# Attention probabilities of a fused two-layer block: turned by way of DRAM and 32x32 blocks instead of on TensorE

## The chip, the cores and the metric

One core of a Trainium2 chip. The metric is the device time of one execution in microseconds (us), as the median over runs. The engines are TensorE (PE in the profile, its weight loads PEld), VectorE (DVE), ScalarE (ACT), GpSimd (POOL) and SyncE (SP, which here only issues DMA).

## What is computed

Two layers over 1024 tokens (16 sequences of 64) of width 512, everything in fp32. Cut to what matters, the reference is:

```python
x = x + L0_xattn(layernorm(x), ctx, ctx)        # linear attention, 8-wide heads
x = x + L0_ffn(layernorm(x))                    # low-rank gated FFN
x = x + L1_xattn(layernorm(x), ctx)             # 16 heads of 96, 4 KV heads, 64 queries x 128 keys
x = x + L1_ffn(layernorm(x))                    # 16 experts, top 4, and a shared expert
# L1_xattn, per sequence b:
scores = einsum("bkgqd,bksd->bkgqs", q, k) / sqrt(96)
attn   = softmax(scores, axis=-1)
out    = einsum("bkgqs,bksd->bkgqd", attn, v)
return out_rows @ Wo.T
```

The change lies in L1_xattn, between the softmax and the product with the values.

## The kernel before, in words

All engines walk through one list of steps, `prog` (lines 296 to 420), and each emits its own part of each step, in the list's order. There is no scheduler at run time: what stands ahead of a wait on an engine delays what stands behind it.

The second attention is cut into 32 **units** n = 2b + hf: sequence b, half hf of the KV heads, that is 8 heads of 64 queries and 128 keys as four 128x128 tiles u. One turn of the loop at line 389, here called iteration n, puts these steps in this order:

```python
("s", n); ("gate_v", ..); ("kv", ..) for n < 7; ("sh_gu", ..) for n in 25, 29, 32
("pn", n); ("q", q + 1, r // 2) for even n < 24; way(n, 0)
("t", n - 1); way(n, 2); ("pv", n - 2); way(n, 1)
```

- `s` (n): TensorE multiplies queries and keys into PSUM bank 2 or 3 (L1451). VectorE takes the row maxima (L1114, L1116), ScalarE the exponentials with their row sums (L798, four instructions) into `prob`.
- `pn` (n): VectorE inverts the sums and multiplies (L907, L908).
- `t` (n - 1), one iteration later: TensorE turns the four 128x128 tiles of `prob` (L1458, through the helper line L1273) into a PSUM bank, and ScalarE copies the bank to `probT` (L803 to L806, helper line L700).
- `pv` (n - 2), two iterations after the scores: TensorE multiplies the values with `probT` (L1466, L1467) into bank 6. VectorE copies the product to `oT` with two copies of 96x192 (L1130) and three of 32x128 (L1132).
- `kv` (L1362 to L1371) projects keys and values in iterations 0 to 6. TensorE waits there until ScalarE has copied the previous projection (L1345; copies L758 to L765).
- `q` (L1433 to L1437) projects queries. ScalarE copies three heads (L789), VectorE the fourth (L1105).
- `way` (L370 to L384) spreads the output projection (`op0`, `opm`, `op1`, L1482), the third layer norm (`ln_stat`, `ln_z`; for five of eight token blocks VectorE turns 32x32 blocks, L1078, and ScalarE moves them, `ln_m`, 16 copies of 32x128 at L743), the router (`gate`, `gate_v`) and the placing of rows (`place`) over later iterations.
- `sh_gu` is the shared expert's first product. Its first one, in iteration 25, waits for the weights `wsh` (L1513).

SP's queue in this stage: it loads `wo` in two halves (L536, L538), then waits until all of Q is done (`s_q`, L539) and loads `wsh` (L540, 1.5 MB). It waits for the router's first result, and for all scores (L544), and loads the first two experts' weights (L546, helper line L443); then it waits for the placed rows and loads the first block of them (L455).

The second layer norm of the layer before is already turned by way of DRAM (`turn_rows`, L516 to L525): SP stores 128 rows (L519), waits for the store to land, and issues four loads of 64 KB that put each quarter of the columns onto its own 32 partitions (L524), and VectorE turns 32x32 blocks (L1083).

After the list, a loop over some 36 blocks of rows runs the experts.

Of the kernel before, what the change touches and what calls it, by code (L numbers as in the profile page):

```python
# [13 lines left out]
P = 128  # L14
# [24 lines left out]
def build(nc, x_d, ctx_d, ctxT_d, cst_d, u1_d, v1_d, u2_d, v2_d, b1_d, b2_d,  # L39
# [7 lines left out]

    id_d = nc.dram_tensor("slots", (P, 2 * P), F32, kind="Internal").ap()

    with ExitStack() as stack:  # L50
# [8 lines left out]
        cst = sb("cst", [P, 4 * P + 224])  # L59
# [9 lines left out]
        c0 = 4 * P  # L69
# [12 lines left out]
        prob = r1[:, 6144:7168].rearrange("p (n u s) -> p n u s", n=2, u=4)  # L82
# [87 lines left out]
        idrow = sb("idrow", [P, P, 2])  # L170
# [69 lines left out]
        s_pn = sem("probs_done")  # L240
        s_o = sem("pv_done")
# [187 lines left out]
        TRN = order(("a_t", "ln_t", "t", "gate", "front", "place", "count"))  # L429
# [44 lines left out]
        def _(sp):  # L474
# [22 lines left out]
            sp.dma_start(cst[:, 2 * P:], cst_d[:, 2 * P:]).then_inc(s_tables, 16)  # L497
# [39 lines left out]
            sp.wait_ge(s_pr, len(KVN))  # L537
            load_wo(1)  # L538
            sp.wait_ge(s_q, 4 * G)  # L539
            sp.dma_start(wsh, ws_d).then_inc(s_ws, 16)  # L540
# [29 lines left out]
        def _(pool):  # L570
# [27 lines left out]
            for step in prog:  # L598
                if step[0] == "a_stat":
                    root(step[1])  # L600
                elif step == ("f_in", 0):
                    pool.wait_ge(s_tables, 16)
                    pool.tensor_copy(counters[:, :], cst[:, 2 * P:4 * P]).then_inc(s_cb, 1)
                elif step[0] == "x1":
                    j = step[1]
                    pool.wait_ge(s_ac, j + 1)
                    pool.tensor_tensor(xr[:, j, :], xr[:, j, :], sout, ALU.add).then_inc(s_x1, 1)
                elif step[0] == "ln_stat":
                    root(J * step[1] + step[2])
                    if step[1] == 3 and step[2] >= J - 2:  # L610
                        place_ids(step[2] - 2)
                elif step[0] == "ln_z" and step[1] == 1:
                    j = step[2]
                    if j == 0:
                        pool.wait_ge(s_ffw, 6 * 16)
                    pool.wait_ge(s_z, LNN[step] + 1)
                    pool.tensor_tensor(xr[:, j, :], xr[:, j, :], b2, ALU.add).then_inc(s_xb, 1)
                elif step[0] == "place":
                    j = step[1]
                    pool.wait_ge(s_sl, j + 1)  # L620
                    if j == 0:
                        pool.wait_ge(s_idz, 16)
                        pool.wait_ge(s_fill, 5 * 16)
                    pool.wait_ge(s_z, LNN[("ln_z", 3, j)] + 1)
                    for k in range(TOPK):
                        if j:
                            pool.wait_ge(s_zs[k], 16 * j)
# [59 lines left out]
        def _(act):  # L687
# [15 lines left out]
            for step in prog:  # L703
# [88 lines left out]
                elif kind == "s":  # L792
                    n = step[1]
                    act.wait_ge(s_snm, n + 1)
                    if n >= 2:
                        act.wait_ge(s_tr, TRN[("t", n - 2)] + 1)
                    for u in range(4):
                        e = act.activation(prob[:, n % 2, u, :], ps[:, 2 + n % 2, u * P:(u + 1) * P], ACT.Exp,  # L798
# [3 lines left out]
                elif kind == "t":  # L802
                    n = step[1]  # L803
                    if n >= 2:
                        act.wait_ge(s_o, n - 1)
                    copied(step, probT[:, n % 2, :])  # L806
# [89 lines left out]
        def _(dve):  # L896
# [7 lines left out]
            def probs(n):  # L904
# [3 lines left out]
                dve.tensor_tensor(prob[:, n % 2, :, :], prob[:, n % 2, :, :],  # L908
                                  srs[:, n % 4, :].rearrange("p (u a) -> p u a", a=1).to_broadcast((P, 4, P)),
# [92 lines left out]
            for step in prog:  # L1002
# [116 lines left out]
                elif kind == "pv":  # L1119
                    n = step[1]  # L1120
                    b, hf = divmod(n, 2)
                    j = b // 2
                    side = slice(S * (b % 2), S * (b % 2) + S)
                    dve.wait_ge(s_o, n + 1)
                    if j >= 2 and b % 2 == 0 and hf == 0:
                        dve.wait_ge(s_op, j - 1)
                    src = ps[:, 6, :].rearrange("p (g h q) -> p g h q", g=2, h=HG)
                    dst = oT[:, j % 2, 6 * hf:6 * hf + 6, side].rearrange("p (g t) q -> p g t q", g=2)
                    for g in range(2):
                        dve.tensor_copy(dst[0:HD, g, :, :], src[0:HD, g, 0:3, :])  # L1130
                    for t in range(3):
                        c = dve.tensor_copy(dst[HD:P, :, t, :], src[32 * t:32 * t + 32, :, 3, :])  # L1132
                    c.then_inc(s_oc, 1)
# [4 lines left out]
                elif kind == "gate_v":  # L1138
                    j = step[1]
                    if j == 0:  # L1140
                        dve.wait_ge(s_small, 32)
                        dve.wait_ge(s_tables, 16)
# [108 lines left out]
        def _(pe):  # L1251
# [55 lines left out]
            for step in prog:  # L1307
# [147 lines left out]
                elif kind == "t":  # L1455
                    n = step[1]
                    pe.wait_ge(s_pn, n + 1)
                    transposes(tbank(step), prob[:, n % 2, :, :].rearrange("p u s -> p (u s)"), 4).then_inc(s_tr, 1)  # L1458
                elif kind == "pv":
                    n = step[1]  # L1460
                    b, hf = divmod(n, 2)
                    pe.wait_ge(s_trc, TRN[("t", n)] + 1)
# [249 lines left out]
```

## Time and profile before

| what | value |
|---|---|
| median of 3 runs | 677.14 us (676.71 to 677.41) |
| the profiled execution | 677.72 us, its span 675.9 us |
| instructions | 9767 |
| PE busy | 662.4 us, 98% |
| DVE busy | 335.7 us, 50% |
| ACT busy | 220.1 us, 33% |
| POOL busy | 175.6 us, 26% |
| chain that ended last | PE 86%, DMA 4%, issue 3%, DVE 2% |
| DMA moved | 103.19 MB, 153 GB/s on average |

Busy time is the union of an engine's instructions. The chain that ended last follows the execution back from its end, at each step to what released it. Times inside the trace count from the span's start. The second attention runs from about 182 us (scores of unit 0) to 428 us (values of unit 31). Each time stands for one profiled execution, 0.58 us above the median.

### The profile page before, as it was taken

Reading aid. Unit: us, or ns where it says so; the run is one execution under the profiler, and the core shown is the slowest. Engines: PE = TensorE matmul, PEld = TensorE weight load, DVE = VectorE, ACT = ScalarE, POOL = GpSimd, SP = SyncE. Lnnn points to the kernel's source line nnn. Section 1 sums busy time; section 2 is a strip of 40 time slices with the busy share of each in tenths; the row PEclk is TensorE's granted clock in tenths of the full one; section 3 lists DMA queues with packets and bytes.
Section 4 is the critical chain, followed back from the end, with each engine's and each line's share of the span. In section 5 each row is a group of like instructions: output and inputs, shape, how many; then the busy total and the mean of one; then the engine's idle time right before and its main releaser. Section 6 shows DMA issues by size and latency. Waiting matters only on the chain.

```text
span 675.9 us, 9767 instructions
## 1 busy us (share of the span) xinstructions
PE 662.4 (98%) x2399; PEld 393.1 (58%) x2400; DVE 335.7 (50%) x875; ACT 220.1 (33%) x626; POOL 175.6 (26%) x227
## 2 busy tenths in 40 slices
PE   9999999999999999999999999999899999999994
PEld 6565444466777776777776776675344444444442
DVE  3995224534334556586766768465233333333332
ACT  5575522222344433535444463220111111111110
POOL 2366100001000000004314053465124333333244
PEclk9999999999999999999999999999999999999998
DMA  9999999331400200001104014426767749768645
GB/s 339 405 422 420 422 421 436 115 118 52 167 1 0 95 1 0 1 1 63 63 2 155 2 64 160 151 79 188 231 134 144 163 83 202 186 122 235 119 75 71
DMA packets 60404, 103.19 MB, mean 153 GB/s; under 512 B 7200, under 2 KB 32544, under 8 KB 59712
## 3 DMA queue, kind: packets, MB, share of 16 engines
q1 hardware_dynamic: 30320, 73.48, 29.5%
q0 software_dynamic: 8816, 18.00, 13.5%
q10 hardware_dynamic: 21232, 11.28, 5.9%
q8 instruction: 17, 0.28, 0.2%
q14 instruction: 19, 0.16, 0.1%
HBM read 46.60 MB, written 56.26 MB: 152 GB/s over the span
## 4 chain that ended last, share of the span: by engine, by line
PE 86%; DMA 4%; issue 3%; DVE 2%; ACTq 1%; ACT 1%; DVEq 1%; POOLq 1%; POOL 0%; SPq 0%
PE ps L1287 51%; PE ps L1482 12%; PE ps L1451 4%; PE ps L1467 4%; PE ps L1273 4%; DMA out<-rq,sidx 3%; PE ps L1398 3%; PE ps L1399 3%; PE ps L1408 3%; ACTq L449 1%; PE ps L1420 1%; DMA xr<-in_x 1%; PE ps L1334 1%; DVEq L1215 1%; DVE rq L980 1%
## 5 line engine op out<-in xcount | busy, mean ns | idle before, releaser
L1287 PE MATMUL ps<-kv,rq 128*128 x432 | 192.5, 594 | 3.2 <-issue 2.7
L1287 PE MATMUL ps<-zT,r 128*128 128x256 f32 (+1 forms) x552 | 132.5, 395 | 0.1
L1287 PEld LDWEIGHTS ps<-kv,rq 128*128 128x128 f32 x432 | 78.9, 190 | 90.3 <-issue 90.2
L1287 PEld LDWEIGHTS ps<-zT,r 128*128 128x128 f32 x552 | 103.4, 190 | 23.5 <-issue 10.1
L1482 PE MATMUL ps<-r 128*128 128x512 f32 x192 | 85.3, 593 | 0.0
L664 POOL DMA_INDIRECT out<-rq,sidx x36 | 56.6, 1573 | 99.3 <-DMA out<-rq,sidx 61.9
L586 POOL TENSOR_SCALAR ve<-mv 128x1 f32<-128x1 f32 x32 | 7.1, 223 | 260.5 <-DVE mv L1000 260.5
L798 ACT ACTIVATE r<-ps,snm 128x128 f32<-128x128 f32 x128 | 45.2, 365 | 59.7 <-DVE snm L1116 59.5
L1212 DVE TENSOR_TENSOR rq<-ps,rq 128x256 f32<-128x256 f32 x36 | 15.2, 423 | 97.3 <-ACT rq L850 97.3
L1482 PEld LDWEIGHTS ps<-r 128*128 128x128 f32 x192 | 35.1, 190 | 37.8 <-issue 37.8
L850 ACT ACTIVATE rq<-ps 128x256 f32<-128x256 f32 x36 | 13.8, 383 | 122.2 <-PE ps L1287 122.2
L628 POOL DMA_INDIRECT slot_rows<-zrow,sloti x32 | 33.1, 1035 | 59.6 <-DVE sloti L1186 51.7
L1223 DVE TENSOR_SCALAR rq<-ps,wts 128x512 f32<-128x512 f32 x36 | 27.0, 750 | 32.4 <-issue 11.5
L1105 DVE COPY rq<-ps 32x256 f32<-32x256 f32 x48 | 20.5, 427 | 38.8 <-PE ps L1287 38.3
L1092 DVE SCALAR_TENSOR_TENSOR rq<-ps,r,rq 128x512 f32<-128x512 f32 (+1 forms) x22 | 16.4, 750 | 39.9 <-ACT rq L779 39.9
L1451 PE MATMUL ps<-kv,rq 96*128 96x128 f32 x256 | 34.7, 278 | 0.0
L593 POOL DMA_INDIRECT slots<-tokw,sloti x32 | 31.0, 970 | 10.5 <-issue 9.2
L1451 PEld LDWEIGHTS ps<-kv,rq 96*128 96x128 f32 x256 | 32.7, 192 | 1.5
L700 ACT COPY r<-ps 128x512 f32<-128x512 f32 x40 | 23.5, 587 | 30.0 <-PE ps L1273 29.7
L1467 PE MATMUL ps<-r,kv 128*96 128x256 f32 x128 | 32.9, 379 | 0.0
L846 ACT COPY rq<-ps 128x256 f32<-128x256 f32 x36 | 13.4, 372 | 51.7 <-PE ps L1273 50.2
L980 DVE STREAM_TRANSPOSE rq<-rq 128x512 f32<-128x512 f32 x36 | 25.3, 702 | 9.1 <-DMA rq<-slot_rows 9.1
(183 smaller groups left out, 844.2 us busy)
## 6 DMA issues: line engine op xcount, KB each, us to landing
slot_rows<-rq SPq DMA_DIRECT2D x4, 8192.0 KB, 50.5
kv<-in_experts SPq DMA_DIRECT2D x54, 256.0 KB, 4.5
rq<-slot_rows ACTq DMA_DIRECT2D x138, 64.0 KB
r<-in_Wq SPq DMA_DIRECT2D x1, 3072.0 KB, 20.6
r<-in_Wo SPq DMA_DIRECT2D x2, 1536.0 KB, 6.6
r<-in_ctx SPq DMA_DIRECT2D x8, 256.0 KB, 8.2
xr<-in_x SPq DMA_DIRECT2D x8, 256.0 KB, 8.4
second_norm_rows<-zrow SPq DMA_DIRECT2D x8, 256.0 KB, 2.1
```

The costliest lines, as they stand in the source:

```text
L593: pool.indirect_dma_start(out=id_d.rearrange("a (b c) -> (a b) c", c=2), out_offset=bass.IndirectOffsetOnAxis(ap=sloti[:, j, k:k + 1], axi ...
L628: pool.indirect_dma_start(out=slot_d, out_offset=bass.IndirectOffsetOnAxis(ap=sloti[:, j, k:k + 1], axis=0), in_=zrow[:, LNN[("ln_z", 3, j ...
L664: pool.indirect_dma_start(out=out_d, in_=ylast[:, par, :] if last else yrow[:, par, :], in_offset=None, out_offset=bass.IndirectOffsetOnAx ...
L700: act.copy(dst, ps[:, n % 2, :] if len(dst.shape) == 2 else ps[:, n % 2, :].rearrange("p (k t) -> p k t", k=KC)).then_inc(s_trc, 1)
L798: e = act.activation(prob[:, n % 2, u, :], ps[:, 2 + n % 2, u * P:(u + 1) * P], ACT.Exp, bias=snm[:, n % 4, u:u + 1], scale=SCALE, accum_o ...
L980: dve.transpose(xT[:, par, :].rearrange("p (k a j) -> p a k j", k=KC, a=4), xrow[:, par, :].rearrange("p (a k i) -> p a k i", a=4, k=KC)). ...
L1223: dve.tensor_scalar(ylast[:, par, :] if last else yrow[:, par, :], ps[:, 6 + par, :], wts[:, bass.ds(col, 1)], None, ALU.mult).then_inc(s_ ...
L1273: mm = pe.transpose(bank[:, c * P:(c + 1) * P], src[:, c * P:(c + 1) * P], ident)
L1287: mm = pe.matmul(out, lhs(k), rhs(k), start=(k == 0), stop=(k == n - 1))
L1451: mm = pe.matmul(ps[:, 2 + n % 2, u * P:(u + 1) * P], qT[0:HD, q % 2, b % 4, h0:h0 + 2, :].rearrange("p h s -> p (h s)"), kT[0:HD, g, b, : ...
L1467: mm = pe.matmul(ps[0:HD, 6, 256 * g:256 * g + 256], v[:, b, c0:c0 + HD], probT[:, n % 2, 256 * g:256 * g + 256], start=True, stop=True)
L1482: mm = pe.matmul(ps[:, 7, :], oT[:, j % 2, m, :], wo[:, m, :], start=(m == 0), stop=(m == NQT - 1))
```

## The change

Step `t` (n) is no longer a step of TensorE and ScalarE. SP stores the normalised `prob` of unit n to DRAM (256 KB), waits for it to land and for VectorE to be done with the landing tile `late`, and issues four loads (64 KB each, runs of 512 bytes) that exchange the 32-partition blocks with the 128-column blocks. VectorE turns the 32x32 blocks from `late` to `probT` in one instruction, at the place of `t` in the list. `prob` gets another order of columns for this, so the exponentials write four runs of 32 and the multiplication has one more dimension. The five copies of `pv` pass from VectorE to ScalarE. On SP all 32 stores and loads stand behind the first half of `wo` and ahead of the experts' weights; the second half of `wo` is issued ahead of unit 7's store, `wsh` ahead of unit 24's. The constants that lay in `cst` for the counters are loaded into `late` first, with a DMA of their own, and the slot table read late (`idrow`) shares `late`.

```diff
-        prob = r1[:, 6144:7168].rearrange("p (n u s) -> p n u s", n=2, u=4)
+        prob = r1[:, 6144:7168].rearrange("p (n b u i) -> p n b u i", n=2, b=4, u=4)
...
-        idrow = sb("idrow", [P, P, 2])
+        late = sb("late", [P, D])
+        idrow = late[:, 0:2 * P].rearrange("p (a c) -> p a c", c=2)
...
-        TRN = order(("a_t", "ln_t", "t", "gate", "front", "place", "count"))
+        TRN = order(("a_t", "ln_t", "gate", "front", "place", "count"))
...
-            sp.dma_start(cst[:, 2 * P:], cst_d[:, 2 * P:]).then_inc(s_tables, 16)
+            sp.dma_start(late[:, 0:2 * P], cst_d[:, 2 * P:4 * P]).then_inc(s_tables, 16)
+            sp.dma_start(cst[:, 2 * P:], cst_d[:, 4 * P:]).then_inc(s_tables, 16)
...
             load_wo(0)
-            sp.wait_ge(s_pr, len(KVN))
-            load_wo(1)
-            sp.wait_ge(s_q, 4 * G)
-            sp.dma_start(wsh, ws_d).then_inc(s_ws, 16)
+            sp.wait_ge(s_cb, 1)
+            for n in range(NU):
+                if n == len(lat_units[1]):
+                    sp.wait_ge(s_pr, len(KVN))
+                    load_wo(1)
+                if n == 24:
+                    sp.wait_ge(s_q, 4 * G)
+                    sp.dma_start(wsh, ws_d).then_inc(s_ws, 16)
+                sp.wait_ge(s_pn, n + 1)
+                sp.dma_start(prob_d[n % 2], prob[:, n % 2].rearrange("p b u i -> p (b u i)")).then_inc(s_pst[n % 2], 16)
+                if n:
+                    sp.wait_ge(s_ptt, n)
+                sp.wait_ge(s_pst[n % 2], 16 * (n // 2 + 1))
+                for b in range(4):
+                    sp.dma_start(late[b * QD:(b + 1) * QD, :].rearrange("p (a e) -> p a e", a=4),
+                                 pquad_d[n % 2, b, :, :, :]).then_inc(s_pld, 16)
...
# ScalarE
                     if n >= 2:
-                        act.wait_ge(s_tr, TRN[("t", n - 2)] + 1)
+                        act.wait_ge(s_pst[n % 2], 16 * (n // 2))
                     for u in range(4):
-                        e = act.activation(prob[:, n % 2, u, :], ps[:, 2 + n % 2, u * P:(u + 1) * P], ACT.Exp,
+                        e = act.activation(prob[:, n % 2, :, u, :],
+                                           ps[:, 2 + n % 2, u * P:(u + 1) * P].rearrange("p (b i) -> p b i", b=4), ACT.Exp,
...
-                elif kind == "t":
+                elif kind == "pv":
                     n = step[1]
-                    if n >= 2:
-                        act.wait_ge(s_o, n - 1)
-                    copied(step, probT[:, n % 2, :])
...
+                    act.wait_ge(s_o, n + 1)
+                    if j >= 2 and b % 2 == 0 and hf == 0:
+                        act.wait_ge(s_op, j - 1)
...
+                    for g in range(2):
+                        act.copy(dst[0:HD, g, :, :], src[0:HD, g, 0:3, :])
+                    for t in range(3):
+                        c = act.copy(dst[HD:P, :, t, :], src[32 * t:32 * t + 32, :, 3, :])
+                    c.then_inc(s_oc, 1)
...
# VectorE
-                elif kind == "pv":
+                elif kind == "t":
                     n = step[1]
...
+                    dve.wait_ge(s_pld, 64 * (n + 1))
+                    if n >= 2:
+                        dve.wait_ge(s_o, n - 1)
+                    dve.transpose(probT[:, n % 2, :].rearrange("p (u a j) -> p a u j", u=4, a=4),
+                                  late[:, :].rearrange("p (a u i) -> p a u i", a=4, u=4)).then_inc(s_ptt, 1)
...
# TensorE
-                elif kind == "t":
-                    n = step[1]
-                    pe.wait_ge(s_pn, n + 1)
-                    transposes(tbank(step), prob[:, n % 2, :, :].rearrange("p u s -> p (u s)"), 4).then_inc(s_tr, 1)
                 elif kind == "pv":
...
-                    pe.wait_ge(s_trc, TRN[("t", n)] + 1)
+                    pe.wait_ge(s_ptt, n + 1)
```

## Rows read from the trace of the kernel before

**Rows 1.** The page: busy time of PE and the other engines.

```profile
PE 662.4 (98%) x2399; PEld 393.1 (58%) x2400; DVE 335.7 (50%) x875; ACT 220.1 (33%) x626; POOL 175.6 (26%) x227
```

**Rows 2.** Busy time of each engine from 181.7 to 428, four windows summed.

```profile
sum 246.30, PE 246.20 PEld 178.49 DVE 156.77 ACT 112.55 POOL 46.84; mean PE 61.55 PEld 44.62 DVE 39.19 ACT 28.14 POOL 11.71
```

**Rows 3.** Chain that ended last, units 30 and 31: start us, us, what.

```profile
422.50 0.44 PE ps L1273 x4
422.94 0.86 PE ps L1467 x4
423.80 3.45 PE ps L1287 x16
427.26 0.86 PE ps L1467 x4
```

**Rows 4.** The same chain about the second key and value projection.

```profile
192.91 1.50 ACT r L798 x8
...
194.92 0.48 ACT kv L765
...
195.44 8.88 PE ps L1287 x32
204.32 0.44 PE ps L1273 x4
```

**Rows 5.** By line: duration ns min/median/max; turning, the copies that move, ScalarE copies.

```profile
L1083 DVE STREAM_TRANSPOSE zT<-zquad x8: 694/702/714, 127.1 to 183.3; 128x512 f32<-128x512 f32 x8
...
L1130 DVE COPY r<-ps x64: 312/344/355, 205.7 to 428.4; 96x192 f32<-96x192 f32 x64
...
L1132 DVE COPY r<-ps x96: 282/286/291, 206.3 to 429.4; 32x128 f32<-32x128 f32 x96
...
L743 ACT COPY zT<-zquad x80: 292/295/298, 273.3 to 398.9; 32x128 f32<-32x128 f32 x80
...
L765 ACT COPY kv<-ps x16: 473/474/479, 10.6 to 231.5; 64x384 f32<-64x384 f32 x16
```

**Rows 6.** Timeline of one round trip of the second norm; L524's landings.

```profile
170.21 0.43 SPq L519 DMA_DIRECT2D second_norm_rows<-zrow  x1
172.45 1.73 SPq L524 DMA_DIRECT2D zquad<-second_norm_rows  x4
...
175.76 0.71 DVE L1083 STREAM_TRANSPOSE zT<-zquad 128x512 f32<-128x512 f32 x1 [0.30 <-DMA zquad<-second_norm_rows]
...
DMA to landing us min/median/max: 1.8/2.0/3.3
```

**Rows 7.** Shared weights: issue and landing, values' copy, unit 23's probabilities, use.

```profile
356.45 0.33 SPq L540 DMA_DIRECT2D r<-in_shared  x1
...
DMA to landing us min/median/max: 6.2/6.2/6.2
...
358.02 0.62 DVE L1130 COPY r<-ps 96x192 f32<-96x192 f32 x2
...
363.62 0.69 DVE L908 TENSOR_TENSOR r<-r,srs 128x512 f32<-128x512 f32 x1
...
373.27 3.62 PE L1287 MATMUL ps<-zT,r 128*128 128x256 f32 x16
```

**Rows 8.** By line, L476: landing of the two halves of wo.

```profile
DMA to landing us min/median/max: 6.5/6.6/6.7
```

**Rows 9.** SP's queue: the first experts' weights and what it issues next.

```profile
412.65 7.02 SPq L443 DMA_DIRECT2D kv<-in_experts  x12
460.01 1.77 SPq L455 DMA_DIRECT2D rq<-slot_rows  x4
```

**Rows 10.** Chain that ended last: scores of units 27 and 29.

```profile
384.75 0.99 PE ps L1451 x8
...
396.10 0.89 PE ps L1451 x8
```

**Rows 11.** By line, L557: landing of 256 KB stores beside other traffic.

```profile
DMA to landing us min/median/max: 4.8/6.2/7.3
```

More of the change, by code:

```diff
@@ L46, in build @@
     zquad_d = zrow_d.rearrange("n (a j) (b e) -> n b j a e", a=4, b=4)
+    prob_d = nc.dram_tensor("probabilities", (2, P, D), F32, kind="Internal").ap()
+    pquad_d = prob_d.rearrange("n (a j) (b e) -> n b j a e", a=4, b=4)
     id_d = nc.dram_tensor("slots", (P, 2 * P), F32, kind="Internal").ap()
@@ L58, in build @@
         xr = sb("xr", [P, J, D])
-        cst = sb("cst", [P, 4 * P + 224])
+        cst = sb("cst", [P, 2 * P + 224])
         zT = sb("zT", [P, KC, T])
@@ L68, in build @@
         ident, blk8 = (cst[:, i * P:(i + 1) * P] for i in range(2))
-        c0 = 4 * P
+        c0 = 2 * P
         iota16 = cst[:, c0:c0 + 16]
@@ L240, in build @@
         s_pn = sem("probs_done")
+        s_pst = [sem(f"probs_stored{i}") for i in range(2)]
+        s_pld = sem("probs_loaded")
+        s_ptt = sem("probs_turned")
         s_o = sem("pv_done")
@@ L601, in _ @@
                 elif step == ("f_in", 0):
-                    pool.wait_ge(s_tables, 16)
-                    pool.tensor_copy(counters[:, :], cst[:, 2 * P:4 * P]).then_inc(s_cb, 1)
+                    pool.wait_ge(s_tables, 32)
+                    pool.tensor_copy(counters[:, :], late[:, 0:2 * P]).then_inc(s_cb, 1)
                 elif step[0] == "x1":
@@ L801, in _ @@
                     e.then_inc(s_p, 1)
-                elif kind == "t":
+                elif kind == "pv":
                     n = step[1]
-                    if n >= 2:
-                        act.wait_ge(s_o, n - 1)
-                    copied(step, probT[:, n % 2, :])
+                    b, hf = divmod(n, 2)
+                    j = b // 2
+                    side = slice(S * (b % 2), S * (b % 2) + S)
+                    act.wait_ge(s_o, n + 1)
+                    if j >= 2 and b % 2 == 0 and hf == 0:
+                        act.wait_ge(s_op, j - 1)
+                    src = ps[:, 6, :].rearrange("p (g h q) -> p g h q", g=2, h=HG)
+                    dst = oT[:, j % 2, 6 * hf:6 * hf + 6, side].rearrange("p (g t) q -> p g t q", g=2)
+                    for g in range(2):
[3 more added lines that the diff above has]
+                    c.then_inc(s_oc, 1)
                 elif kind == "gate":
@@ L907, in probs @@
                 link(dve.reciprocal(srs[:, n % 4, :], ssum[:, n % 4, :]))
-                dve.tensor_tensor(prob[:, n % 2, :, :], prob[:, n % 2, :, :],
-                                  srs[:, n % 4, :].rearrange("p (u a) -> p u a", a=1).to_broadcast((P, 4, P)),
+                dve.tensor_tensor(prob[:, n % 2], prob[:, n % 2],
+                                  srs[:, n % 4, :].rearrange("p (b u i) -> p b u i", b=1, i=1).to_broadcast((P, 4, 4, QD)),
                                   ALU.mult).then_inc(s_pn, 1)
@@ L1118, in _ @@
                     probs(step[1])
-                elif kind == "pv":
+                elif kind == "t":
                     n = step[1]
[L1121 to L1133, printed above, removed]
+                    dve.wait_ge(s_pld, 64 * (n + 1))
[3 more added lines that the diff above has]
+                                  late[:, :].rearrange("p (a u i) -> p a u i", a=4, u=4)).then_inc(s_ptt, 1)
                 elif kind == "op1":
@@ L1141, in _ @@
                         dve.wait_ge(s_small, 32)
-                        dve.wait_ge(s_tables, 16)
+                        dve.wait_ge(s_tables, 32)
                         dve.wait_ge(s_ms, 3)
```

## The prediction

> **What bounds the kernel now.** I read the page first. PE is busy for 98% of the span, no other engine for more than 50% [rows 1]. Then the windows over the second attention, from the scores of unit 0 to the values of unit 31: PE works 246.20 of 246.30 us, VectorE 156.77, ScalarE 112.55 [rows 2]. So in this stage only what leaves PE's queue can shorten the kernel, and only while nothing new makes PE wait. Then the chain that ended last, because busy time doesn't say what an instruction costs in elapsed time. In it the four transposes of a unit (L1273 x4) take 0.44 us, and the values' matmuls (L1467) start as they end: 422.50 + 0.44 = 422.94 [rows 3]. The last unit shows the same place without transposes between: the shared expert's matmuls start at 423.80, take 3.45, and L1467 starts at 427.26, at once [rows 3]. So taking the transposes out should leave no hole. There is one exception. About the second key and value projection the chain leaves PE and runs through ScalarE: exponentials from 192.91 for 1.50, then the copy of the projection from 194.92 for 0.48, and PE starts at 195.44 [rows 4]. There PE waits for that copy.
>
> **The change, part by part.**
>
> *Transposes off PE.* 32 units of 0.44 us, or 0.435 with the next digit (four of about 109 ns), are 13.9 us. Unit 0's are gone to no use: they lie in iteration 1, just ahead of the PE start at 195.44 which the copy sets [rows 4], and nothing in the change makes that copy earlier. PE will only wait 0.44 us longer there. 31 x 0.435 = **13.5 us gained**.
>
> *Round trip of the probabilities.* The same kernel does such a round trip for the second norm: store issued at 170.21, loads from 172.45 for 1.73, the turn at 175.76 after a wait for the last landing, 0.71 for the turn itself [rows 6]. That is 5.55 us until VectorE can start and 6.3 until the block is turned. What hides it: unit n's probabilities are ready late in iteration n, its values are multiplied at the end of iteration n + 2, so two whole iterations lie between. 246.3 / 32 = 7.7 us is a mean iteration; units 27 to 29 go at (396.10 - 384.75) / 2 = 5.7 us [rows 10], 5.2 once the transposes are gone. Two of the shortest are 10.4 us against 6.3. Only one landing tile exists, so the cycle that repeats is loads, landing, turn: 1.73 + 2.0 + 0.7 = 4.4 us per unit [rows 6], still below 5.2. VectorE will sometimes wait up to a microsecond for a landing; behind it stand the maxima of the next scores, and PE needs their exponentials only an iteration later. I cost the round trip at nothing. If the landings take 3.3 us instead of 2.0, the longest of rows 6, the cycle is 5.7 us, and the few short iterations lose about 0.5 us each: 0 to 3 us in all.
>
> *VectorE.* It gives up 2 x 0.344 + 3 x 0.286 = 1.55 us per unit and takes on a turn of 0.70 [rows 5]. It gains 0.85 us per unit and no longer waits for PE's values before it takes the next maxima. Worth nothing directly, since it doesn't bound.
>
> *ScalarE.* It loses the copy of the turned bank and takes the five copies. 32x128 takes it 0.295 us, 64x384 0.474; between these, 96x192 is about 0.34 [rows 5], so 2 x 0.34 + 3 x 0.295 = 1.57 us. An iteration then has 1.5 of exponentials [rows 4] and 1.57 of copies. For five token blocks `ln_m` adds 16 copies of 0.295 over two iterations, 2.4 us each: 5.4 us, under the mean of 7.3 after the change, over the 5.2 of iterations 27 and 28. PE needs each copy of `pv` an iteration later, so a lag of 0.2 us per iteration is taken up there. Zero, with 0 to 3 us as bounds (at most 0.3 us in each of the ten iterations with `ln_m`). [...]
>
> *SP's queue: wo.* The second half of `wo` is issued behind unit 6's loads instead of as soon as keys and values are done. It lands in 6.6 us [rows 8] and is first read in iteration 9. Hidden by two iterations; without them it would cost those 6.6 us.
>
> *SP's queue: the shared weights.* This is the one place where I expect a new wait. Before, `wsh` was issued at 356.45 and landed in 6.2 us, long before its first reader, the PE group at 373.27 [rows 7]. Now it stands behind unit 23's round trip. On the clock of before, unit 23's probabilities end at 363.62 + 0.69 = 364.3; VectorE comes there about 0.8 us sooner, since the five copies of 358.02 [rows 7] are replaced by one turn, so 363.5. Store to first load is 172.45 - 170.21 = 2.24, the loads 1.75 [rows 6]: `wsh` is issued at 367.5 and lands 6.2 to 6.7 later [rows 7, 8], at 373.7 to 374.2. PE reaches its first reader at 373.27 less three sets of transposes (units 21 to 23), 372.0. So PE waits 1.7 to 2.2 us, **2.0 us lost**, once. From both sides: 0, if SP is two microseconds ahead of this, to 3.5, if small transfers in the same queue slow the load. While `wsh` moves, unit 24's store and loads stand behind it in the queue, so its turn is late by some 3 us; it is read two iterations on, and PE itself waits meanwhile.
>
> *SP's queue: the experts.* They were issued from 412.65 over 7 us, and SP's next transfer was at 460.01 [rows 9]. Now they follow unit 31's loads, some 9 us later. Hidden by the 40 us in which SP did nothing.
>
> *POOL's queue, the extra constant DMA, the order of columns.* POOL keeps its instructions; its copy of the constants waits for one more small load of the opening, far ahead of use. Exponentials and multiplication handle as many elements as before. Nothing, because none of it is ahead of a PE start; bounds -0.5 to +0.5 us.
>
> **Sum.** 13.5 - 2.0 = 11.5 us. The profiled execution would go from 677.72 to 666.2. It lies 0.58 us above the median, 677.14, so the median goes to **665.6 us**.
>
> **The rivals.**
>
> *The shared weights come in time.* If SP is ahead by 2 us at unit 23, only the transposes count: 677.14 - 13.5 = 663.6. For it: the landing and the need are within 2 us of each other. Against: each term has a row. 0.16.
>
> *ScalarE or the landing tile lags in the short iterations.* Both lags at their bounds, 3 us each, take the gain down to 5.5: 671.6; half of it, 668.6. For it: the margins of 5.4 against 5.2 and 4.4 against 5.2. Against: the slack of an iteration behind each. 0.16.
>
> *Slower: the landing tile becomes the bound.* The cycle loads, landing, turn is 2.43 us plus the landing. It equals the mean iteration of 7.7 us at a landing of 5.3 us, and from there the kernel is slower than before. Stores of 256 KB land in 6.2 us where other traffic runs [rows 11]. At 6.2 for each load a unit takes 8.6 us, 0.9 more than before: 32 x 0.9 = 29 us, 706 us. Against: the loads of the second norm have this very shape and land in 2.0, at most 3.3 [rows 6]. The Trainium skill's page "DMA: Bandwidth & Descriptors", section "Latency and other measured facts", says an access to DRAM takes 0.2 us on average and 2 us at high load. By that the landing would be an estimated 3.8 us under load, still short of the turning point. 0.06.
>
> *No change that can be measured*, by several waits that happen to use up the gain: 0.02.
>
> **How the numbers follow.** Forecast, gain of 10 to 13 us: 0.60. A measurement of this kernel can tell about 0.2% from no change, 1.35 us. All cases but the last two are faster by more: 0.60 + 0.16 + 0.16 = 0.92; same 0.02; slower 0.06. The range takes in the no-wait rival and its small bounds below (663.6 - 0.8) and the lagging rival to somewhat above its middle: 662.8 to 669.2.
>
> **What would show it.** In the changed profile: 128 matmuls of L1273 fewer; L1467 starting as the matmuls before it end; the copies of `pv` on ScalarE at about 0.34 and 0.295 us; VectorE's turn 0.70 us; loads landing in about 2.0 us; each iteration 0.44 us shorter from scores to scores. PE's one new wait should stand ahead of the first shared-expert group, for a DMA, about 2 us long, and the wait at the second projection should be 0.4 us longer. I am wrong if PE waits ahead of L1467 for the turn, or if the stage from the first scores to the last values is not 11 to 12 us shorter than 246.3, or if what is gained there is lost behind it.

## The result and the profile after

The changed kernel takes 682.49 us (680.86 to 684.29, 6 runs) against 677.27 us before on the same chip (676.71 to 678.43, 6 runs): ratio 1.0063, 95% interval 1.0049 to 1.0076. It is 0.6% slower where 1.7% faster was forecast. The profiled execution took 683.33 us, its span 681.5, against 677.72 and 675.9 before. Three executions in all the runs below fell into a far slower state (two of the kernel before at 1182 us, one of a variant at 1431 us) and are in no number here.

The page of the changed kernel, busy time by engine; it answers to [rows 1]:

```profile
PE 652.2 (96%) x2271; PEld 381.0 (56%) x2272; DVE 307.0 (45%) x747; ACT 245.0 (36%) x754; POOL 175.1 (26%) x227
```

PE does 128 matmuls fewer (2399 - 2271) and is busy 10.2 us less. The span is 5.6 us longer. So PE now waits where it didn't. What PE waited for in the changed kernel (engine, line, releaser: us in total, times, longest):

```profile
PE ps L1310 <- DMA r<-in_shared: 8.1, 1, 8.1
...
PE ps L1518 <- DVE mcum L1022: 2.6, 2, 1.7
PE ps L1486 <- DVE r L1155: 1.6, 1, 1.6
...
PE ps L1310 <- ACT kv L785: 0.6, 1, 0.6
```

One wait of 8.1 us for the shared weights, two for the routing's `mcum`, which VectorE makes, and one for the turned probabilities. The wait at the second projection is 0.6 us. Where they lie, from PE's timeline of the second attention (all starts with idle before them over 0.6 us):

```profile
321.68 0.18 PE L1518 MATMUL ps<-mask,counters 128*128 128x16 bf16 x1 [1.68 <-DVE mcum L1022]
351.55 0.18 PE L1518 MATMUL ps<-mask,counters 128*128 128x16 bf16 x1 [0.94 <-DVE mcum L1022]
374.64 6.45 PE L1310 MATMUL ps<-zT,r 128*128 128x256 f32 x16 [8.05 <-DMA r<-in_shared]
404.47 1.10 PE L1486 MATMUL ps<-r,kv 128*96 128x256 f32 x4 [1.56 <-DVE r L1155]
```

The group behind the long wait takes 6.45 us; the same 16 matmuls took 3.62 [rows 7]. The windows show why (length, busy time and count of PE, PEld, DVE, ACT, POOL, granted clock, DMA share, GB/s):

```profile
366.00:372.00 6.00, 0.59 (x6) 0.40 (x4) 3.24 (x8) 5.11 (x21) 0.95 (x1) 0.83 0.80 280
372.00:375.00 3.00, 0.35 (x1) 0.36 (x2) 0.52 (x1) 0.00 (x0) 0.00 (x0) 0.50 0.06 10
```

PE does nothing from 366.6 on. Within this wait the granted clock falls: its mean is 0.83 from 366 to 372 and 0.50, which is 1.2 of 2.4 GHz, from 372 on. The group that took 6.45 us began at this level. The shared weights thus cost 8.05 + 2.83 = 10.9 us. The second row holds something else: from 372 to 374.6 the DMA engines move next to nothing (share 0.00 from 373), and yet the load counts as landed only at 374.64.

SP's queue shows why the load was late:

```profile
299.64 1.73 SPq L559 DMA_DIRECT2D late<-probabilities  x4
...
308.00 1.78 SPq L559 DMA_DIRECT2D late<-probabilities  x4
311.59 0.34 SPq L554 DMA_DIRECT2D probabilities<-r  x1
321.01 1.73 SPq L559 DMA_DIRECT2D late<-probabilities  x4
323.31 0.34 SPq L554 DMA_DIRECT2D probabilities<-r  x1
325.67 1.75 SPq L559 DMA_DIRECT2D late<-probabilities  x4
...
359.90 0.34 SPq L554 DMA_DIRECT2D probabilities<-r  x1
361.95 1.78 SPq L559 DMA_DIRECT2D late<-probabilities  x4
363.78 0.43 SPq L552 DMA_DIRECT2D r<-in_shared  x1
366.87 0.34 SPq L554 DMA_DIRECT2D probabilities<-r  x1
376.02 1.74 SPq L559 DMA_DIRECT2D late<-probabilities  x4
```

From store (L554) to loads (L559) it is 2.0 to 2.4 us in 18 of 32 units, as 2.24 in [rows 6], but 9.4 us after 311.59 and 9.2 after 366.87. In four early units, not shown, it is 6.3 to 7.3 us, because SP waits there for VectorE's turn in the one landing tile; no wait of PE comes of these. GpSimd's queue at the first of these: the last of the four scatters of rows, then the first and last of the four that write a token's slot number and weight, 8 bytes to a row:

```profile
306.36 0.96 POOL L648 DMA_INDIRECT slot_rows<-zrow,sloti  x1 [0.30 <-issue]
307.62 0.96 POOL L613 DMA_INDIRECT slots<-tokw,sloti  x1 [0.30 <-issue]
...
311.41 0.98 POOL L613 DMA_INDIRECT slots<-tokw,sloti  x1 [0.30 <-issue]
```

The four id scatters of the third block run on GpSimd from 362.27 to 367.0, up to the store of 366.87; this store also stands behind the shared weights' load in SP's queue. VectorE's side, the turn by line (count, busy us, mean ns, then idle before it), and ScalarE's copies by line (ns min/median/max):

```profile
L1155 DVE STREAM_TRANSPOSE r<-late 128x512 f32<-128x512 f32 x32 | 22.5, 705 | 22.0 <-DMA late<-probabilities 21.6
```

```profile
L834 ACT COPY r<-ps x64: 312/319/340, 205.4 to 433.6; 96x192 f32<-96x192 f32 x64
...
L836 ACT COPY r<-ps x96: 254/256/259, 206.0 to 434.4; 32x128 f32<-32x128 f32 x96
```

The turn takes its forecast 0.70 us, but VectorE stands 21.6 us waiting for landings. The longest of these waits, 6.91 us, lies behind the loads of 376.02. The five copies take 2 x 0.319 + 3 x 0.256 = 1.41 us, less than the 1.57 forecast.

### The profile page after: what moved, and what is told of

It is laid out like the page before. It is cut to its first block, busy times and chain, and to the rows that moved or that the text cites. A ratio compares the mean times of both kernels' runs of the same rounds, so it can differ in the third digit from the quotient of the medians.

```text
span 681.5 us, 9672 instructions
## 1 busy us (share of the span) xinstructions
PE 652.2 (96%) x2271; PEld 381.0 (56%) x2272; DVE 307.0 (45%) x747; ACT 245.0 (36%) x754; POOL 175.1 (26%) x227
## 4 chain that ended last, share of the span: by engine, by line
PE 67%; DMA 15%; issue 6%; DVE 5%; SPq 2%; ACT 2%; ACTq 1%; POOLq 1%; another core or an unknown queue 1%; POOL 0%; DVEq 0%
PE ps L1310 45%; DMA out<-rq,sidx 8%; PE ps L1501 5%; PE ps L1421 3%; PE ps L1431 3%; PE ps L1422 3%; DMA late<-probabilities 2%; PE ps L1486 2%; PE ps L1474 2%; DMA probabilities<-r 2%; SPq L559 2%; PE ps L1296 2%; DMA r<-in_shared 2%; PE ps L1443 1%; DMA xr<-in_x 1%
## 5 line engine op out<-in xcount | busy, mean ns | idle before, releaser
L1310 PE MATMUL ps<-zT,r 128*128 128x256 f32 (+1 forms) x552 | 135.3, 401 | 8.6 <-DMA r<-in_shared 8.1
L1310 PEld LDWEIGHTS ps<-zT,r 128*128 128x128 f32 x552 | 105.4, 194 | 33.0 <-issue 10.1
L1155 DVE STREAM_TRANSPOSE r<-late 128x512 f32<-128x512 f32 x32 | 22.5, 705 | 22.0 <-DMA late<-probabilities 21.6
L1011 DVE STREAM_TRANSPOSE rq<-rq 128x512 f32<-128x512 f32 x36 | 25.2, 701 | 10.8 <-DMA rq<-slot_rows 10.8
```

Source lines behind the costliest of these rows:

```text
L1011: dve.transpose(xT[:, par, :].rearrange("p (k a j) -> p a k j", k=KC, a=4), xrow[:, par, :].rearrange("p (a k i) -> p a k i", a=4, k=KC)). ...
L1155: dve.transpose(probT[:, n % 2, :].rearrange("p (u a j) -> p a u j", u=4, a=4), late[:, :].rearrange("p (a u i) -> p a u i", a=4, u=4)).th ...
L1310: mm = pe.matmul(out, lhs(k), rhs(k), start=(k == 0), stop=(k == n - 1))
```

## The experiments

The theory: the round trip is no hidden cost. Beside GpSimd's 8-byte scatters it takes 5 to 9 us to land what takes 2 elsewhere; VectorE stands in order behind them, and the shared weights, in the same queue, come late. Rivals: the copies on ScalarE, the single landing tile, the single queue, the large load itself.

In what follows "last values" is the start of the last weight load of the values' matmuls. It is 427.5 before and 430.0 after, from a common start near 182, so the stage is 2.5 us longer; the other 3.1 of the 5.6 us are outside.

**Shared weights one unit sooner.**

```
-                if n == 24:
+                if n == 23:
                     sp.wait_ge(s_q, 4 * G)
                     sp.dma_start(wsh, ws_d).then_inc(s_ws, 16)
```

> The changed kernel with the shared weights' load one place further up in SP's queue: ahead of unit 23's store, not ahead of unit 24's. In the changed kernel PE waits 8.05 us for this load and then runs its next group in 6.45 us in place of 3.62, 10.9 us together. Theory Q (the load's place in SP's queue is what turns the gain into a loss): issued some 6 us sooner, about 357.5, it lands at 364 to 368; the wait falls to 0 to 2 us, the slow group goes, and the time falls by 8 to 11 us, to 671 to 675, faster than before the change. Theory L (landings are slow because other traffic is in flight, wherever the load stands): the load meets the row scatters from 356.7 and still takes 10 us or more, PE waits 3 us or more, and less than 6 us come back, 677 or more. Theory S (the copies moved to ScalarE cost the time): at most 2 us change.

678.58 us (674.64 to 680.33, 10 runs), ratio 1.0001 (0.9982 to 1.0021). The waits and SP's queue of the profiled execution, the fastest of the ten:

```profile
PE ps L1486 <- DVE r L1155: 5.1, 2, 4.3
```

```profile
353.22 0.43 SPq L552 DMA_DIRECT2D r<-in_shared  x1
356.09 0.34 SPq L554 DMA_DIRECT2D probabilities<-r  x1
365.62 1.74 SPq L559 DMA_DIRECT2D late<-probabilities  x4
```

The wait for the weights is gone. But now the store behind them takes 9.5 us to its loads, and PE waits for the turn. Last values at 424.1, 5.9 us sooner than in the change, whose median is 3.9 us higher. So of the 10.9 us, some come back as a new wait. The wait for the weights went, as theory Q said, but the median lies in the range of theory L, 677 or more.

**The copies back on VectorE** (the round trip stays).

```
# moved from ScalarE's program to VectorE's
-                            act.copy(dst[0:HD, g, :, :], src[0:HD, g, 0:3, :])
+                            dve.tensor_copy(dst[0:HD, g, :, :], src[0:HD, g, 0:3, :])
```

> The changed kernel with the five copies of each unit's values back on VectorE, the turning through DRAM kept. Theory S (moved copies): ScalarE's waits with no visible reason at 431 and 434 and its late copy of positions go, and 2 to 4 us come back, 679 to 680. Theory Q and theory L: VectorE has 1.55 us more per unit, so the shared weights' load is issued about 1 us later still and each wait for a landing falls on a fuller engine; the time stays or rises by 1 to 4 us, 682 to 686.

694.47 us (692.93 to 697.81, 4 runs), ratio 1.0236 (1.0209 to 1.0264): 12 us worse than the change.

```profile
PE ps L1310 <- DMA r<-in_shared: 9.6, 1, 9.6
PE ps L1486 <- DVE r L1155: 7.5, 5, 3.7
PE ps L1518 <- DVE mcum L1007: 4.4, 2, 2.7
```

That is outside both expectations. VectorE's time is not free once it also waits for landings. Handing the copies to ScalarE is what keeps the loss small.

**The ids placed at the end.** The 8-byte scatters of the first four blocks are issued with the last ones.

```
-                    if j < J - 4:
-                        place_ids(j)
...
+            for j in range(J - 4):
+                place_ids(j)
             place_ids(J - 2)
```

> The changed kernel with GpSimd's 8-byte scatters of slot ids for the first four token blocks moved from the attention stage to the end of its placing work; the row scatters stay. It will be slower in all, since 16 more scatters of 1.27 us stand ahead of the id table (10 to 20 us), so the attention stage alone is read: last values' matmul at 429.6 us in the changed kernel. Theory L in the form that the small scatters slow the landings (loads issued at 308.0 landed at 317.2, at 397.3 in 6.3 us, the store of 337.0 in 5.4 us, each beside such scatters): those landings fall to 2 to 3 us, PE's waits of 1.68 and 0.94 us for the expert mask go, the shared weights land in 7 us, and the last values start at 420 to 424. If the row scatters (256 KB each) do it, landings and stage stay within 1 us of what they were. Theory Q alone: the wait for the shared weights stays at 6 us or more.

696.25 us in its one run, for a reason of its own: at the end of the stage PE waits 21.7 us for the slots, which the scatters now write so late. The stage before that is what the run was for:

```profile
PE ps L1629 <- DMA late<-slots: 21.7, 1, 21.7
PE ps L1314 <- DMA r<-in_shared: 1.9, 1, 1.9
```

```profile
365.20 5.41 PE L1314 MATMUL ps<-zT,r 128*128 128x256 f32 x16 [1.90 <-DMA r<-in_shared]
```

```profile
311.29 0.34 SPq L554 DMA_DIRECT2D probabilities<-r  x1
313.65 1.74 SPq L559 DMA_DIRECT2D late<-probabilities  x4
...
358.25 0.43 SPq L552 DMA_DIRECT2D r<-in_shared  x1
```

The store that took 9.4 us takes 2.4. SP waits 56.0 us for its stores in all, against 72.7 in the change; VectorE waits 7.4 us for landings against 21.6. The shared weights are issued at 358.25 and land in 6.9 us, and PE waits 1.9 us for them, as forecast (2.0). But the group behind this wait takes 5.41 us instead of 3.62, at a granted clock of 0.62 from 366 to 368, so the place costs 3.7 us in all. The store behind the load, at 361.31, takes 4.6 us to its loads with no id scatter beside it. No wait for `mcum`, none for the turn. Last values at 417.8, 12.2 us ahead of the change and 9.7 ahead of before.

**No round trip.** VectorE turns its own probabilities; the exchange of blocks between partitions is left out, and with it stores and loads. The copies stay on ScalarE.

```
-                    dve.wait_ge(s_pld, 64 * (n + 1))
+                    dve.wait_ge(s_pn, n + 1)
...
-                                  late[:, :].rearrange("p (a u i) -> p a u i", a=4, u=4)).then_inc(s_ptt, 1)
+                                  prob[:, n % 2]).then_inc(s_ptt, 1)
```

> The changed kernel without the round trip: VectorE turns the 32x32 blocks straight from the probabilities, nothing goes through DRAM, and SP loads the shared weights and the experts where the kernel before does. It leaves out the exchange of blocks between partitions, so the attention's values are others and the router may choose other experts; the attention stage is what is read. This is the gain of the transposes alone with ScalarE's copies kept. Forecast of the prediction's first term: last values' matmul 31 x 0.435 = 13.5 us sooner than the 427.1 of before, at 413.6 +-0.5, no PE wait for the shared weights. Theory S: ScalarE's copies take 2 us or more of it, 415.6 or later. Theories Q and L: all of the loss was in the DMA path, 413.6.

664.04 us in its one run, 13.7 below the profiled 677.72. Last values at 414.2, 13.3 ahead of before. This is the term of the transposes, 13.5, alone. ScalarE's copies and VectorE's turn take nothing from it.

**Two landing tiles, the turn an iteration later**, on top of the weights one unit sooner. The second tile takes the place of three tensors that are dead or moved.

```
-                    sp.wait_ge(s_ptt, n)
+                    sp.wait_ge(s_ptt, n - 1)
...
-            if 1 <= n <= NU:
-                prog.append(("t", n - 1))
+            if 2 <= n <= NU:
+                prog.append(("t", n - 2))
```

> The changed kernel with three things of the round trip relaxed: two landing tiles in place of one, VectorE's turn of a unit placed behind the maxima of the scores two units on (not behind the next unit's probabilities), and the shared weights issued ahead of unit 23's store. A landing then has 10 us or more from its issue before VectorE stands still, where it had about 5. Theory L+Q (small scatters stretch landings to 6 to 9 us, and the one tile and the early turn let them reach PE): all PE waits for the turn, for the expert mask and for the shared weights go or fall below 1 us each, last values' matmul at 414 to 417 us, time 664.5 to 668. If the landings' own length bounds the stage whatever the order (a unit's cycle over 7 us), the stage stays at 424 us or later and the time at 674 or more.

674.74 us (672.74 to 679.8, 12 runs), ratio 0.9953 (0.9931 to 0.9975): faster than before, by half a per cent. The theory's 664.5 to 668 was missed; the time lies where the expectation's other case has it (674 or more), with last values at 423.6. Two waits for the turn are left, the longer 4.3 us, behind the shared weights as in the first experiment. So the tile and the order account for 3 to 4 us of its 678.58, not for the rest.

**The kernel before, its shared weights held back.** No round trip at all.

```
             sp.wait_ge(s_q, 4 * G)
+            sp.wait_ge(s_pn, 24)
             sp.dma_start(wsh, ws_d).then_inc(s_ws, 16)
```

> The kernel before, with one wait more on SP: the shared weights' load is held until unit 23's probabilities are ready (364.3 us), so that it runs beside the row scatters (361.2 to 366.4) and the 8-byte scatters of slot ids (366.7 to 371.5). Nothing goes through DRAM for the probabilities here. Theory L: the landing takes 8 to 11 us in place of 6.2, at 372 to 375, and PE waits 0 to 2 us ahead of the group of 373.3. If the 10.8 us of the changed kernel came from the loads and stores of the probabilities in the same queue, it lands in 6.2 to 7 us, at 371, and PE doesn't wait.

677.46 us in its one run. The load was issued at 364.39, beside the id scatters, and PE did not wait at 373.27. So it landed in under 8.9 us. The share of the DMA engines is 0.81 to 1.03 until 372 and 0.11 in the microsecond after; if the last of these bytes were the load's, it took over 7.6 us, against 6.2 before. That fits neither expectation: it doesn't show the 8 us of the one, nor exclude them. The scatters alone don't make 10.8.

**The kernel before, its copies on ScalarE.**

```
# moved from VectorE's program to ScalarE's
-                            dve.tensor_copy(dst[0:HD, g, :, :], src[0:HD, g, 0:3, :])
+                            act.copy(dst[0:HD, g, :, :], src[0:HD, g, 0:3, :])
```

> The kernel before with one part of the change alone: the five copies of a unit's values on ScalarE, TensorE still turning the probabilities and ScalarE still copying the turned bank. VectorE has 1.55 us less per unit, ScalarE 1.33 more. Prediction's view (neither bounds): within 0.5 us of before. Theory S: 1 to 4 us slower, with PE waits for ScalarE in iterations with the moved blocks.

678.68 us (677.35 to 680.09, 9 runs), ratio 0.9998 (0.9986 to 1.001). Alone, this half of the change is worth nothing and costs nothing.

**Shared weights on ScalarE's queue**, on top of the two tiles.

```
+                    if (q, g) == (3, 3):
+                        act.dma_start(wsh, ws_d).then_inc(s_ws, 16)
```

> The version with two landing tiles and the later turn, with the shared weights' load issued on ScalarE's queue after its copy of the last queries, so that no store or load of the probabilities stands behind it. In the two-tile version unit 23's store was issued at 354.59 behind it and its loads came at 365.43; PE waited 4.31 us for that turn and ran at half clock after it. Theory Q (order within one queue): store and loads pass beside the big load, the 4.31 us and the slow stretch after it (5.0 us, groups of 1.75, 1.73, 2.06 and 4.69 us in place of 1.03, 0.96, 1.14 and 3.60) go, 7 to 9 us come back, last values at 415 us, time 666 to 668. If the DMA engines' own throughput is what the transfers share (both queues end in the same engines), the store lands late all the same, PE still waits 2 to 4 us, and the time is 671 to 675.

672.56 us (670.43 to 674.64, 6 runs), ratio 0.9913 (0.9891 to 0.9935). The load is now issued at 347.71. The store beside it, of 348.12, takes 7.4 us to its loads, with no id scatter beside it. The 10.8 us of the two-tile version are no fair comparison: that store stood behind the load in the same queue and beside the id scatters. One long wait is left:

```profile
357.44 0.47 SPq L553 DMA_DIRECT2D probabilities<-r  x1
362.00 5.32 SPq L558 DMA_DIRECT2D late<-probabilities  x4
```

```profile
369.61 2.01 PE L1487 MATMUL ps<-r,kv 128*96 128x256 f32 x4 [2.79 <-DVE r L1156]
```

The median came out where sharing of the DMA engines was expected, 671 to 675, not the queue alone, 666 to 668. It doesn't show sharing by itself, because the wait that is left lies behind a store beside the id scatters (the last experiment); the store of 348.12 does. The Trainium skill says of queues (page "DMA: Bandwidth & Descriptors", section "Issuing engines are not separate DMA queues") that transfers of the scalar, sync and gpsimd engines run on the same 16 DMA engines and interleave. The trace agrees, with 7.4 us beside the load where a store takes 2.0 to 2.4 elsewhere.

**The same, with one tile**: the change itself with the load in another queue, and so also issued sooner.

```
-                if n == 24:
-                    sp.wait_ge(s_q, 4 * G)
-                    sp.dma_start(wsh, ws_d).then_inc(s_ws, 16)
...
+                    if (q, g) == (3, 3):
+                        act.dma_start(wsh, ws_d).then_inc(s_ws, 16)
```

> The changed kernel, one landing tile as in the change, with only the shared weights moved to ScalarE's queue, behind the last query copy (about 350 us). Theory, both the queue and the shared DMA engines count: the 10.9 us at the shared expert's group go, but the trips of units 22 to 24 run beside the load and take 7 to 9 us each, and with one tile PE waits 3 to 5 us once for the turn there and runs a few groups at half clock: 675 to 679 us, no faster than the kernel before. Rival, the single queue alone was the trouble: store to loads stays at 2.4 us for these units, PE waits for no turn, and the time is 670 to 672 us.

675.64 us (673.2 to 678.89, 10 runs), ratio 0.9966 (0.9943 to 0.999). In the range of the theory, but for another wait than it named:

```profile
PE ps L1517 <- DVE mcum L1021: 4.2, 4, 2.6
...
PE ps L1485 <- DVE r L1154: 1.0, 2, 0.5
```

What is late is `mcum`, 2.6 us once: the work that stands behind VectorE's wait for a landing. The L1500 group behind it takes 5.29 us instead of 3.60. And the kernel is faster than before, which the theory didn't say. Moving one load turns the change from 0.6% slower to 0.3% faster. It starts at 349.34 instead of 363.78, in another queue; starting it at 353.22 in SP's queue gave 1.0001. Between these two lie both the queue and 3.9 us, and no run tells them apart.

**Wide scatters in place of the small ones.** The ids at the end, and at their old place four more scatters per block, of rows of 2 KB into a spare tensor.

```
+                    if j < J - 4:
+                        for k in range(TOPK):
...
+                            pool.indirect_dma_start(
+                                out=spare_d, out_offset=bass.IndirectOffsetOnAxis(ap=sloti[:, j, k:k + 1], axis=0),
+                                in_=wo[:, 0, :], in_offset=None).then_inc(s_sp[k], 16)
```

> As the version with GpSimd's scatters of slot ids for the first four token blocks moved to the end, but at their old place four more scatters per token block of 2 KB rows go to a spare tensor in DRAM (128 descriptors each as well, the source a row block of wo; the spare tensor is read by nothing). The time in all is again longer for the scatters at the end; the attention stage is read. Theory L1 (the 8-byte size of the writes delays other landings): the loads issued at about 308 and 340 land in 2 to 3.5 us as in the version without the small scatters, shared weights in 7 to 9 us, last values at 418 to 422. Theory L2 (any further indirect scatter on GpSimd's queue does, by its descriptors): loads and stores beside them take 6 to 9 us as in the changed kernel, last values at 426 or later.

700.35 us in its one run, again with a long wait for the slots at the end. In the stage:

```profile
311.29 0.34 SPq L556 DMA_DIRECT2D probabilities<-r  x1
314.33 1.74 SPq L561 DMA_DIRECT2D late<-probabilities  x4
...
358.55 0.46 SPq L554 DMA_DIRECT2D r<-in_shared  x1
361.61 0.34 SPq L556 DMA_DIRECT2D probabilities<-r  x1
369.63 1.74 SPq L561 DMA_DIRECT2D late<-probabilities  x4
```

As many scatters in the same place, each moving 256 times the bytes, and the store takes 3.0 us where the 8-byte ones made 9.4. So it is not that a scatter runs there but that its writes are so small; or that they lie close together, since the 8-byte rows fill a table of 128 KB and the wide ones a large tensor, which no run tells apart. The shared weights do suffer from the wide ones: they land in 9.6 us instead of 6.9, PE waits 4.8 us, the store behind the load takes 8.0 us, and last values are at 422.2 instead of 417.8, just outside the 418 to 422 expected.

**The third block's ids later**, on top of two tiles and ScalarE's queue. They now go with the fourth block's.

```
-                    if j < J - 4:
-                        place_ids(j)
+                    if j in (0, 1):
+                        place_ids(j)
+                    if j == 3:
+                        place_ids(2)
+                        place_ids(3)
```

> The two-tile kernel with the shared weights on ScalarE's queue, with one thing changed: the four 8-byte id scatters of the third token block, which fell on the store of 357.44 us, are held back to those of the fourth block (about 390 us), which then are eight. Theory, the 8-byte writes stretch the landings: the store that took 4.6 us to its loads takes 2 to 3 us, PE's 2.79 us wait ahead of the values' matmuls at 369.6 and the half clock behind it are gone, and last values end 4 to 6 us sooner up to there; at the eight scatters the wait for the turn grows from 1.3 to 3 to 5 us. Together 669 to 673 us. Rival, the 1.5 MB load beside them stretches the landings: the wait at 369.6 stays over 2 us, and the time is 673 to 676 us.

671.52 us (668.75 to 672.82, 4 runs), ratio 0.9886 (0.9853 to 0.992). SP's queue at the same store, and PE's waits:

```profile
357.18 0.45 SPq L553 DMA_DIRECT2D probabilities<-r  x1
360.00 1.73 SPq L558 DMA_DIRECT2D late<-probabilities  x4
```

```profile
PE ps L1318 <- DVE rq L1019: 2.0, 1, 2.0
PE ps L1494 <- issue: 1.8, 1, 1.8
PE ps L1557 <- DVE cols L966: 1.2, 1, 1.2
```

The store that took 4.6 us takes 2.8, its loads are issued in 1.7 us instead of 5.3, and PE no longer waits for any turn by name. Beside the eight scatters a store now takes 5.6 us to its loads (386.35 to 391.91), and the 1.8 us that the profile puts down to issue lie ahead of values at 390.30; if they are that stretch's price, it is under the 3 to 5 us expected. Last values at 417.4, 10.1 ahead of before and 4.4 ahead of the previous version. Its time is 1.0 us below that one's, less than the two intervals tell apart: the rest is given back after the stage. This is the fastest version found, 7 us under the kernel before.

## Why the prediction was wrong

*Transposes off PE:* right. 13.5 us forecast; 13.7 measured where nothing else was in the way.

*ScalarE and VectorE's own work:* right. Copies of 1.41 us per unit, nothing lost with them on ScalarE alone. A copy of 32x128 takes 256 ns there and one of 96x192 takes 319.

*The wait at the second projection:* right, 0.27 us before, 0.6 now.

*Experts and the second half of `wo`:* hidden, as said. No wait of PE for either.

*Round trip costed at nothing:* this step failed. The working took the landings from a place where no GpSimd scatter runs [rows 6] and set them against the iteration. Beside the id scatters of the four blocks the store takes 9.4, 5.5, 9.2 (this one also behind the shared weights) and 4.7 us to its loads, and loads issued by 309.78 hold VectorE until 317.22. VectorE then stands, and what is queued behind is the maxima, the gate's work and the next probabilities. PE pays 1.68 + 0.94 for `mcum`, 1.56 for the turn. The slack of an iteration that I counted on covered single landings of 2 to 3 us, as the runs without id scatters show (no such wait), but not these. I had named the landing tile as a slower rival and priced it for all 32 units; what happened was four places, and no bound on the cycle. The flaw was to weigh "in every unit" against "nowhere".

*Shared weights, 2.0 us, at most 3.5:* mis-sized; it measured 10.9. By its own terms: issued at 363.78 where the forecast, on this kernel's clock, was about 358.8, so 5.0 later, because unit 23's probabilities were ready only at 359.9; PE itself 3.3 later than forecast; landing after 10.8 us instead of 6.5. Then 2.0 + 5.0 - 3.3 + 4.3 = 8.0, and 8.05 was measured. The clock's fall after it, 2.83 us, was in no term. That omission is a fault of its own: without the small scatters PE waits 1.9 us here, as forecast, and still loses 1.8 more in the group behind, 3.7 in all and over the bound of 3.5.

The sum for the stage: 13.3 gained (the longer wait at the projection is already in it), less 10.9, 2.6 and 1.6, is 1.8 lost; measured 2.5, so 0.7 us have no name. With the ids at the end it closes: 13.3 - 3.7 = 9.6, measured 9.7.

*Outside the stage* the changed kernel loses 3.1 us (681.5 - 430.0 = 251.5 from the last values to the end, against 248.4). From 430 on PE's waits before matmuls add up to 5.7 us (0.68 for `zT`, 1.09, 0.44, 1.57, 1.37, 0.55) against 3.5 before (1.56, 1.13, 0.25, 0.55). So 2.2 of the 3.1 are there, at the hand-over to the experts. Without a round trip this part was as short as before: 662.2 - 414.2 = 248.0 us against 248.4, though with other probabilities and so perhaps other experts. It is 248.7 with the weights one unit sooner, and 250.7 in the kernel before with its copies on ScalarE, so a round trip need not cost it, and a version without one loses most of it too. No run tried it apart, and its cause stays open. In the best version it is 4.4 us.

Open as well is how 8-byte writes delay the completion of others. It is no lack of throughput. The windows of the changed kernel behind the first block's scatters (columns as above, DMA share last but one):

```profile
316.00:318.00 2.00, 2.00 (x11) 1.77 (x10) 0.78 (x2) 0.00 (x0) 0.00 (x0) 1.00 0.02 7
318.00:320.00 2.00, 2.00 (x10) 1.31 (x8) 1.86 (x7) 0.45 (x3) 0.80 (x2) 1.00 0.00 0
```

The DMA engines are all but idle, and the store of 311.59 still isn't counted as landed; its loads go out at 321.01. The Trainium skill states two things that could bear on it. "DMA: Bandwidth & Descriptors", section "Specifications", says that below 512 bytes an engine does a read-modify-write; the section "Latency and other measured facts" gives 2 us for an access to DRAM at high load. The landing that the prediction estimates from the second, 3.8 us, is under the 7.4 us from the end of the loads' issue at 309.78 to 317.22; no run here shows the first at work.

## What to carry to other kernels

A landing time read in one stage is not the price in another: before a transfer goes into a loop, list what the other queues do beside it, above all scatters of a few bytes, and take the duration from there. A round trip on an in-order engine costs what stands behind its wait, not only what reads its result. When a move pushes a large load behind such a trip, give it a queue and a time of its own first: here the two together were worth 1%. And a wait of PE costs more than its length where the clock falls in it: 1.8 us more on top of 1.9, 2.83 on top of 8.05.

## What the runs showed of the hardware

- Beside four scatters of 8 bytes to a row, a 256 KB store in the changed kernel takes 4.7 to 9.4 us (store issue to first load) where 2.0 to 2.4 is usual; beside scatters of 2 KB rows 2.7 to 3.7. These are places without the 1.5 MB load.
- Transfers can be counted as landed after the DMA engines have gone idle: the store of 311.59 wasn't counted as landed at 320, though the DMA engines' share was 0.02 from 316 and 0.00 from 318; the shared weights were released at 374.64, with a share of 0.00 from 373. In the best version a store of 386.35 beside eight id scatters waits until 391.91, with a share of 0.03 and 0.01 from 388 on.
- The 1.5 MB load lands in 6.2 us (before) to 6.9 us (ids at the end), in 9.6 beside wide scatters and in 10.8 beside small ones, the last three with a store behind it. In the same queue this store takes 4.6 us without id scatters, 8.0 beside wide ones and 9.2 to 10.8 beside small ones; in another queue, with no id scatters beside it, 4.5 to 7.4.
- After waits of 1.90, 2.60, 2.79, 4.3 and 8.05 us TensorE's groups ran for a few us in part or whole at the lower of its two levels (values' matmuls 2.0 us instead of 1.03 or 1.10); after the waits of 1.56 and 1.68 us in the changed kernel they did not.
- Four transposes of 128x128 in a row cost TensorE 0.435 us, and their removal gave that back, 13.3 us in the stage for 31 sets on the path.
